# Layer norm of six attention samples by products with a constant tile instead of token rows

## The chip, the cores and the metric

One Trainium2 chip, one core of it. The time is the device time of one execution in microseconds. Five engines work in their own instruction streams and wait for each other by semaphores: PE (TensorE: matmuls and transposes), DVE (VectorE), ACT (ScalarE), POOL (GpSimd) and SyncE, whose queue issues the DMAs.

## The reference

Eight samples of 512 tokens with 512 features go through four blocks: a rotation, two modulated linear layers with a norm over the whole sample, a low-rank steering, and a transformer layer (attention with 16 heads of 32, then a feed-forward of 2048). The change touches the first norm of the last block:

```python
def layernorm(x, gamma, beta):
    mu = jnp.mean(x, axis=-1, keepdims=True)
    var = jnp.var(x, axis=-1, keepdims=True)
    return (x - mu) * jax.lax.rsqrt(var + EPS) * gamma + beta
h = layernorm(x, gamma1, beta1)
Q = (h @ Wq + bq).reshape(B, T, N_HEADS, D_HEAD).transpose(0, 2, 1, 3)
...
attn = jax.nn.softmax(scores, axis=-1)
ctx = jnp.einsum('bhqk,bhkd->bhqd', attn, V)
```

## The kernel before

A sample lies in SBUF as four tiles `x[:, j, :]` of 128 features (partitions) by 512 tokens. The norm's sums run over features, across partitions. So PE turns the sample (`tokens_in`, 16 transposes 128x128 in four groups), ACT copies the token rows out (`tokens_out`), DVE computes mean and variance (`statistics`: bn_stats, bn_aggr), POOL the reciprocal root (`prepare_rstd`), DVE normalises (`normalise`), PE turns back (`tokens_back`, four groups), ACT multiplies by gamma and adds beta (`scale_back`), and POOL cuts the result into two fp32r halves (`split`), which the three-pass products for Q, K and V read.

Attention runs over 32 groups n of four heads, four to a sample b = n // 4, two groups to a step: `first_steps(n, b)` for groups 0 and 1 of a sample, `last_steps(n, b)` for 2 and 3. In them each engine's order is written out by hand, and the norm of sample b + 1 is woven in. For a unit u of 12 in a group, PE makes scores (`score`), DVE adds the mask and takes maxima (`max_unit`), ACT takes exponentials with their sums (`exponentials`). For the transposed scores, PE makes `score_by_key`, ACT `exponentials_by_key`, POOL zeroes what is masked (`cut_later(n, half)`, four selects), PE multiplies with the values (`context`). `score_by_key(n, u)` waits for `exponentials_by_key(n, u - 2)`.

Q, K (`qk_piece`), V (`v_piece`), the steering (`st`), turned tiles (`tin`, `tb`) and the output projection share two PSUM banks. `BANK_ORDER` lists their uses in turn, even places in one bank and odd places in the other; `claim` waits until the use two places before has been taken out. DVE takes Q and K out by `qk_out` (`qk_high`, then `qk_low`). `qk_high` of the Q tile also waits for the stack DMAs of the group before (`wait_stack`), which read the tile it overwrites. SyncE's queue issues per group, in order: `max_rows(n - 1, 1)`, `stack_rows(n + 1, (0, 1))`, for group 0 `steered_out(b + 1)` (1 MB), `max_rows(n, 0)`, `stack_rows(n + 1, (2, 3))`, each `stack_rows` six DMAs.

## Time and profile before

| | us |
|---|---|
| median of 3 runs | 1609.07 |
| lowest, highest | 1608.97, 1609.23 |
| span of the profiled execution | 1610.9 |
| attention, one sample in the steady part | 82.55 |

The span runs from the first to the last instruction of one profiled execution. PE is matmuls, whose ends are modelled, so starts are the safer reading; PEld is weight loads. Steady attention lies between about 327 and 823 us, five whole samples of 82.55 us.

### The profile page before, as it was taken

How to read it: one execution, taken by the hardware profiler on the slowest of the kernel's cores; microseconds unless marked ns; L12 is line 12 of the kernel's file. 1: busy time of each engine (PE TensorE's matmuls, PEld its weight loads, DVE VectorE, ACT ScalarE, POOL GpSimd, SP SyncE). 2: the span in 40 equal slices, each digit the busy share in tenths (PEclk: the TensorE clock that was granted, in tenths of full speed). 3: DMA queues.
4: the chain of work that ended last, by engine and by line, in shares of the span. 5: the costliest groups of instructions: out<-in, count | busy, mean ns of one | idle time of the engine just before them, and what ended most of it. 6: DMA issues, size and time to landing. Idle time of an engine off the chain costs nothing.

```text
span 1610.9 us, 27177 instructions
## 1 busy us (share of the span) xinstructions
PE 1585.8 (98%) x9296; PEld 1299.5 (81%) x9298; DVE 1166.6 (72%) x2767; ACT 982.8 (61%) x2331; POOL 410.9 (26%) x605
## 2 busy tenths in 40 slices
PE   7999999999999999999999999999999999999999
PEld 4688786777777777777777688898999999999998
DVE  7999888786969686868778576785655656565643
ACT  6888766887878787878778755352433324242422
POOL 8998810313222313131312110201010110202010
PEclk8999999999999999999999999999999999999999
DMA  7042135543545444444337435866464555556361
GB/s 308 0 183 97 66 126 126 149 130 92 138 95 139 100 115 122 111 116 115 88 90 214 167 152 207 303 262 232 178 234 170 213 225 188 212 178 265 142 211 68
DMA packets 62257, 254.79 MB, mean 158 GB/s; under 512 B 10628, under 2 KB 16004, under 8 KB 46760
## 3 DMA queue, kind: packets, MB, share of 16 engines
q1 hardware_dynamic: 62120, 253.06, 48.2%
q8 instruction: 74, 1.21, 0.3%
q14 instruction: 63, 0.52, 0.1%
HBM read 153.93 MB, written 48.23 MB: 125 GB/s over the span
## 4 chain that ended last, share of the span: by engine, by line
PE 90%; POOL 3%; DMA 2%; DVE 2%; ACT 1%; issue 1%; SPq 1%; POOLq 0%; DVEq 0%; ACTq 0%
PE psum L83 24%; PE psum L84 23%; PE psum L85 23%; PE psum L1529 5%; PE psum L1549 5%; PE psum L1579 4%; PE psum L1470 1%; DMA k_weights<-w_factors 1%; PE psum L1478 1%; PE psum L2451 1%; DMA k_raw<-in_t_w 1%; POOL k_gs_square L252 1%; POOL k_gs_root L247 1%; ACT psum L1229 1%; POOL k_gs_scaled L256 1%
## 5 line engine op out<-in xcount | busy, mean ns | idle before, releaser
L1229 ACT ACTIVATE psum<-psum,b_mx 128x512 f32<-128x512 f32 (+3 forms) x512 | 258.9, 509 | 63.2 <-DVE b_mx L990 62.0
L990 DVE CUSTOM_DVE_ANT_0 psum<-psum,b_mask 128x512 f32<-128x512 f32 (+3 forms) x512 | 244.7, 506 | 53.0 <-PE psum L1529 48.1
L2398 ACT ACTIVATE k_act<-k_stack_f,k_smalls 128x512 f32<-128x512 f32 x112 | 80.9, 722 | 303.6 <-DVE k_stack_f L2237 297.1
L1241 ACT ACTIVATE k_exps<-psum 128x512 f32<-128x512 f32 (+1 forms) x384 | 194.6, 532 | 59.4 <-PE psum L1549 58.1
L864 POOL TENSOR_SCALAR_AFFINE_SELECT k_exps<-k_exps 128x256 f32<-128x256 f32 x256 | 96.4, 413 | 381.0 <-ACT k_exps L1241 379.1
L2097 POOL TENSOR_SCALAR k_result<-k_result,k_pb 128x512 f32<-128x512 f32 x32 | 59.2, 1866 | 434.9 <-DVE k_result L2156 434.9
L2216 DVE TENSOR_TENSOR k_act_lo<-k_act,k_act_hi 128x512 fp32r<-128x512 f32 x112 | 77.2, 690 | 120.6 <-ACT k_act_hi L2401 120.6
L83 PE MATMUL psum<-k_act_hi,k_w_hi 128*128 128x512 f32 x384 | 150.8, 393 | 0.0
L84 PE MATMUL psum<-k_act_lo,k_w_hi 128*128 128x512 f32 x384 | 150.5, 392 | 0.0
L85 PE MATMUL psum<-k_act_hi,k_w_lo 128*128 128x512 f32 x384 | 150.2, 391 | 0.0
L2237 DVE TENSOR_TENSOR k_raw<-psum,k_raw 128x256 f32<-128x256 f32 x168 | 70.5, 421 | 106.0 <-PE psum L85 95.4
L1529 PE MATMUL psum<-k_stack 96*128 96x512 f32 (+3 forms) x512 | 142.6, 330 | 3.1 <-DMA k_stack<-k_samples 2.0
L85 PE MATMUL psum<-k_normed,k_weights 128*128 128x512 f32 (+1 forms) x384 | 144.3, 376 | 0.0
L1549 PE MATMUL psum<-k_stack 98*128 98x512 f32 (+3 forms) x512 | 134.8, 332 | 0.6 <-ACT k_exps L1241 0.3
L83 PE MATMUL psum<-k_normed,k_weights 128*128 128x512 f32 (+1 forms) x320 | 126.0, 394 | 0.0
L84 PE MATMUL psum<-k_normed,k_weights 128*128 128x512 f32 (+1 forms) x320 | 120.0, 375 | 0.0
L1529 PEld LDWEIGHTS psum<-k_stack 96*128 96x128 f32 x512 | 93.6, 190 | 29.9 <-issue 8.8
L1549 PEld LDWEIGHTS psum<-k_stack 98*128 98x128 f32 x512 | 91.0, 189 | 27.7 <-issue 9.6
L1229 ACT ACTIVATION_READ_ACCUMULATOR psum<-psum,b_mx 128x1 f32 x512 | 108.6, 212 | 0.0
L85 PEld LDWEIGHTS psum<-k_act_hi,k_w_lo 128*128 128x128 f32 x384 | 72.1, 188 | 16.2
L85 PEld LDWEIGHTS psum<-k_normed,k_weights 128*128 128x128 f32 x384 | 73.0, 190 | 14.1
L83 PE MATMUL psum<-k_h,k_stack 128*128 128x256 f32 x294 | 82.6, 281 | 0.0
(372 smaller groups left out, 4418.2 us busy)
## 6 DMA issues: line engine op xcount, KB each, us to landing
k_stack<-w_factors SPq DMA_DIRECT2D x35, 1792.0 KB, 7.7
k_stack<-k_samples SPq DMA_DIRECT2D x384, 128.0 KB, 2.4
k_weights<-w_factors SPq DMA_DIRECT2D x17, 1792.0 KB, 7.5
x<-k_tokens SPq DMA_DIRECT2D x10, 1024.0 KB, 4.3
k_tokens<-x SPq DMA_DIRECT2D x8, 1024.0 KB, 5.1
d<-k_result SPq DMA_DIRECT2D x32, 256.0 KB, 2.9
k_raw<-x SPq DMA_DIRECT2D x8, 1024.0 KB, 4.8
k_raw<-d SPq DMA_DIRECT2D x8, 1024.0 KB, 7.1
```

The lines of the kernel that those rows point to most:

```text
L83: pe.matmul(out, w_hi, x_hi, start=start and k == 0, stop=False)
L84: pe.matmul(out, w_hi, x_lo, start=False, stop=False)
L85: last = pe.matmul(out, w_lo, x_hi, start=False, stop=stop and k == n - 1)
L864: pool.affine_select(out=own, in_=own, compare_op=ALU.is_ge, fill=0.0, base=0, pattern=[[0, 2], [1, P]], channel_multiplier=-1).then_inc(c ...
L990: last = dve.tensor_tensor_reduce(got, got, mask[:, S - width:S], -INV_SQRT_DH, -2.0 * MASKED, ALU.add, ALU.min, mx[n % 2][:, h, t:t + 1])
L1229: act.activation(sc(n, u)[:, at:at + width], sc(n, u)[:, at:at + width], ACT.Exp, bias=mx[n % 2][:, h, t:t + 1], scale=-1.0, accum_out=sum ...
L1241: act.activation(exps[n % 2][:, h, at:at + width], by_key(n, u)[:, 0:width], ACT.Exp, scale=INV_SQRT_DH).then_inc(k_act, 1)
L1529: last = pe.matmul(sc(n, u)[:, at:at + width], stack[n % 2][0:3 * DH, 2 * h, t * P:(t + 1) * P], stack[n % 2][0:3 * DH, 2 * h + 1, 0:width ...
L1549: last = pe.matmul(by_key(n, u)[:, at:at + width], stack[n % 2][0:3 * DH + 2, 2 * h + 1, j * P:(j + 1) * P], stack[n % 2][0:3 * DH + 2, 2 ...
L2216: dve.tensor_tensor(act_lo[n % 2], act_f[:], act_hi[n % 2].bitcast(F32), ALU.subtract).then_inc(act_lo_set, 1)
L2237: dve.tensor_tensor(out, got, other, ALU.add).then_inc(partial_set, 1)
L2398: act.activation(act_f[:], whole_tile, ACT.Gelu, bias=small(smalls, "b1", 2 * pair % M + second)).then_inc(pair_gelu, 1)
```

## The change

For samples 2 to 7 (`SPREAD`) the sample stays as it is. POOL adds the four feature tiles (`sample_sum`) and cuts the sum into two fp32r halves; two products with the constant tile `mean_of`, all elements 1/512, leave the mean of each token in every partition of a bank (`mean_product`). DVE subtracts it from the four tiles (`centre`), ACT squares (`squares`), POOL adds and cuts again (`square_sum`), two products give the variance (`variance_product`), ACT takes a rough reciprocal root by logarithm and exponential (`rough_rstd`), DVE makes one Newton step of it (`refine`, three instructions 128x512) and multiplies the four tiles (`multiply`), ACT applies gamma and beta (`scale_spread`), POOL splits (`split_spread`). The last norm before feed-forward and samples 0 and 1 are as before. `sample_in(b + 2)` moves from group 1 to the end of group 2 on SyncE's queue.

```diff
 BANK_ORDER = (
     (("q", 0, 1), ("k", 0, 1), ("st", 1, 0), ("v", 0, 0), ("st", 1, 1), ("st", 1, 2), ("st", 1, 3), ("v", 0, 1),
-     ("tin", 1, 0), ("q", 0, 2), ("k", 0, 2), ("tin", 1, 1), ("tin", 1, 2), ("tin", 1, 3), ("v", 0, 3),
+     ("q", 0, 2), ("mean", 1, 0), ("k", 0, 2), ("v", 0, 3), ("var", 1, 0),
      ("v", 0, 2)),
-    (("tb", 1, 0), ("q", 0, 3), ("k", 0, 3), ("tb", 1, 1), ("tb", 1, 2), ("wo", -1, 0), ("tb", 1, 3),
-     ("wo", -1, 1), ("q", 1, 0), ("k", 1, 0), ("wo", -1, 2), ("wo", -1, 3), ("pt", 2, 0), ("p", 2, 0)),
+    (("q", 0, 3), ("k", 0, 3), ("wo", -1, 0), ("wo", -1, 1), ("q", 1, 0), ("k", 1, 0), ("wo", -1, 2), ("wo", -1, 3), ("pt", 2, 0), ("p", 2, 0)),
 )
...
                 if g == 0 and b + 1 < B:
                     steered_out(b + 1)
-                if g == 1 and b + 2 < B:
-                    sample_in(b + 2)
                 if g == 3:
                     attention_out(b - 1, 2)
                 max_rows(n, 0)
                 if g == 2:
                     attention_out(b - 1, 0)
                 stack_rows(n + 1, (2, 3))
+                if g == 2 and b + 2 < B:
+                    sample_in(b + 2)
 
...
+
+        def sample_sum(b):
+
+            wait_taken(pool, ("st", b, 1))
+            pool.wait_ge(xl_set, J * b)
+            pool.tensor_tensor(tok[:, 0, :], x[:, 0, :], x[:, 1, :], ALU.add).then_inc(mean_sums, 1)
+            for j in (2, 3):
+                wait_taken(pool, ("st", b, j))
+                wait_sums(pool, b, j - 1)
+                pool.tensor_tensor(tok[:, 0, :], tok[:, 0, :], x[:, j, :], ALU.add).then_inc(mean_sums, 1)
+            wait_sums(pool, b, 3)
+            pool.tensor_copy(sums_r[:, 0, :], tok[:, 0, :]).then_inc(mean_sums, 1)
+            wait_sums(pool, b, 4)
+            pool.tensor_tensor(sums_r[:, 1, :], tok[:, 0, :], sums_r[:, 0, :].bitcast(F32), ALU.subtract).then_inc(mean_sums, 1)
+
+        def square_sum(b):
+
+            wait_squares(pool, b, 2)
+            pool.tensor_tensor(x[:, 0, :], x[:, 0, :], x[:, 1, :], ALU.add).then_inc(mean_sums, 1)
+            for j in (2, 3):
+                wait_squares(pool, b, j + 1)
+                wait_sums(pool, b, 4 + j)
+                pool.tensor_tensor(x[:, 0, :], x[:, 0, :], x[:, j, :], ALU.add).then_inc(mean_sums, 1)
+            wait_sums(pool, b, 8)
+            pool.tensor_copy(squares_r[:, 0, :], x[:, 0, :]).then_inc(mean_sums, 1)
+            wait_sums(pool, b, 9)
+            pool.tensor_tensor(squares_r[:, 1, :], x[:, 0, :], squares_r[:, 0, :].bitcast(F32), ALU.subtract).then_inc(mean_sums, 1)
+
+        def split_spread(b, j):
+            wait_squares(pool, b, J + 2 + j + 1)
+            if j == 0:
+                wait_full(pool, ("k", b - 1, G - 1))
+                wait_full(pool, ("v", b - 1, V_TILES[1][-1]))
+            pool.tensor_copy(xh[:, j, :], tok[:, j, :]).then_inc(xh_set, 1)
+            pool.wait_ge(xh_set, J * b + j + 1)
+            pool.tensor_tensor(xl[:, j, :], tok[:, j, :], xh[:, j, :].bitcast(F32), ALU.subtract).then_inc(xl_set, 1)
 
         def split(b, j):
...
                 if g == 2 and b + 1 < B:
                     for j in range(J):
-                        split(b + 1, j)
+                        split_spread(b + 1, j)
                 cut_later(n - 1, 0)
+                if g == 0 and b + 1 < B:
+                    sample_sum(b + 1)
                 if g == 1 and b + 1 < B:
-                    prepare_rstd(b + 1)
-
-        return steps(prepare_rstd, split, stacked_ones, cut_later, mask_and_low, slots)
+                    square_sum(b + 1)
+
+        return steps(prepare_rstd, mean_constants, split, stacked_ones, cut_later, mask_and_low, slots)
...
+        def centre(b, j):
+            wait_full(dve, ("mean", b, 0))
+            dve.tensor_tensor(tok[:, j, :], x[:, j, :], pj(("mean", b, 0)), ALU.subtract).then_inc(
+                mean_out if j < J - 1 else pj_dve, 1)
+
+        def refine(b):
+
+            bank, y, step = pj(("var", b, 0)), x[:, 3, :], x[:, 0, :]
+            wait_squares(dve, b, J + 2)
+            dve.scalar_tensor_tensor(step, bank, LN_EPS, y, ALU.add, ALU.mult).then_inc(pj_dve, 1)
+            wait_taken(dve, ("var", b, 0))
+            dve.scalar_tensor_tensor(step, step, -0.5, y, ALU.mult, ALU.mult).then_inc(mean_out, 1)
+            wait_spread(dve, b, J)
+            dve.scalar_tensor_tensor(step, step, 1.5, y, ALU.add, ALU.mult).then_inc(mean_out, 1)
+
+        def multiply(b, j):
+
+            wait_spread(dve, b, J + 1)
+            dve.tensor_tensor(tok[:, j, :], tok[:, j, :], x[:, 0, :], ALU.mult).then_inc(mean_out, 1)
 
...
             for k in range(3):
                 max_unit(n + 1, k)
+            shift_rows(n, 1)
+            max_unit(n + 1, 3)
+            qk_out(n + 2, 0)
+            max_unit(n + 1, 4)
             if b + 1 < B:
-                statistics(b + 1, 0)
-            shift_rows(n, 1)
-            for k in range(3, 6):
-                max_unit(n + 1, k)
+                centre(b + 1, 0)
+                centre(b + 1, 1)
+            max_unit(n + 1, 5)
             maxima_out(n, 1)
+            if b + 1 < B:
+                centre(b + 1, 2)
+                centre(b + 1, 3)
             max_unit(n + 1, 6)
             max_unit(n + 1, 7)
             shift_rows(n + 1, 0)
-            qk_out(n + 2, 0)
             qk_out(n + 2, 1)
             max_unit(n + 1, 8)
             max_unit(n + 1, 9)
-            if b + 1 < B:
-                for k in range(1, 4):
-                    statistics(b + 1, k)
             ctx_low(n - 1)
             max_unit(n + 1, 10)
             maxima_out(n + 1, 0)
-            if b + 1 < B:
-                normalise(b + 1, 0)
-                normalise(b + 1, 1)
+            values_out(b, 3)
             max_unit(n + 1, 11)
             if b + 1 < B:
-                normalise(b + 1, 2)
-                normalise(b + 1, 3)
-            values_out(b, 3)
+                refine(b + 1)
 
...
             values_out(b, 2)
             max_unit(n, 0)
             shift_rows(n - 1, 1)
-            for k in range(1, 5):
-                max_unit(n, k)
+            multiply(b + 1, 0)
+            max_unit(n, 1)
+            multiply(b + 1, 1)
+            max_unit(n, 2)
+            multiply(b + 1, 2)
+            max_unit(n, 3)
+            multiply(b + 1, 3)
+            max_unit(n, 4)
             maxima_out(n - 1, 1)
             for k in range(5, 8):
...
+        def squares(b, j):
+            if j < J - 1:
+                wait_spread(act, b, j + 1)
+            else:
+                wait_taken(act, ("mean", b, 0))
+            if j == 0:
+                act.wait_ge(x2_st, 16 * (b + 1))
+            act.activation(x[:, j, :], tok[:, j, :], ACT.Square).then_inc(mean_act, 1)
+
+        def rough_rstd(b):
+
+            y = x[:, 3, :]
+            wait_full(act, ("var", b, 0))
+            act.wait_ge(mask_made, 5)
+            wait_sums(act, b, 8)
+            act.activation(y, pj(("var", b, 0)), ACT.Ln, bias=eps[:]).then_inc(mean_act, 1)
+            wait_squares(act, b, J + 1)
+            act.activation(y, y, ACT.Exp, scale=-0.5).then_inc(mean_act, 1)
+
+        def scale_spread(b, j):
+            wait_normalised(act, b, j + 1)
+            act.activation(tok[:, j, :], tok[:, j, :], ACT.Identity, bias=small(smalls, "beta1", j),
+                           scale=small(smalls, "gamma1", j)).then_inc(mean_act, 1)
...
+            if b + 1 < B:
+                squares(b + 1, 0)
+                squares(b + 1, 1)
+                squares(b + 1, 2)
             log_sums(n + 1, 0)
             exponentials(n + 1, 6)
+            if b + 1 < B:
+                squares(b + 1, 3)
             exponentials(n + 1, 7)
-            for k in range(2, 5):
+            for k in range(2, 6):
                 exponentials_by_key(n, k)
-            if b + 1 < B:
-                tokens_out(b + 1, 1)
-            exponentials_by_key(n, 5)
-            if b + 1 < B:
...
+            exponentials_by_key(n, 9)
+            if b + 1 < B:
+                rough_rstd(b + 1)
+            exponentials_by_key(n, 10)
...
+            scale_spread(b + 1, 0)
+            exponentials(n, 3)
+            scale_spread(b + 1, 1)
+            exponentials(n, 4)
+            scale_spread(b + 1, 2)
+            exponentials(n, 5)
+            scale_spread(b + 1, 3)
...
+        def mean_product(b):
+            if b == SPREAD[0]:
+                pe.wait_ge(mask_made, 6)
+            wait_sums(pe, b, 5)
+            out = claim(("mean", b, 0))
+            pe.matmul(out, mean_of[:], sums_r[:, 0, :], start=True, stop=False)
+            pe.matmul(out, mean_of[:], sums_r[:, 1, :], start=False, stop=True).then_inc(pj_full, 1)
+
+        def variance_product(b):
+            wait_sums(pe, b, 10)
+            out = claim(("var", b, 0))
+            pe.matmul(out, mean_of[:], squares_r[:, 0, :], start=True, stop=False)
+            pe.matmul(out, mean_of[:], squares_r[:, 1, :], start=False, stop=True).then_inc(pj_full, 1)
...
-            if b + 1 < B:
-                tokens_in(b + 1, 0)
...
             score(n + 1, 3)
             qk_piece(b, 2, 3)
+            if b + 1 < B:
+                mean_product(b + 1)
...
-            if b + 1 < B:
-                tokens_in(b + 1, 1)
             score(n + 1, 9)
...
             score_by_key(n, 9)
+            if b + 1 < B:
+                variance_product(b + 1)
             v_piece(b, 2, 0)
...
             score(n, 0)
             score(n, 1)
-            tokens_back(b + 1, 0)
             score(n, 2)
...
```

Three places show how orders moved. All are in the first step of the second sample with the steady order.

DVE before, from `max_unit(n + 1, 6)` on (L990 is max_unit, L1070 shift_rows, L1002 and L1035 qk_out):

```order
L990 ISA psum,b_mx<-psum,b_mask 128x384 [waits b_s_full]
L990 ISA b_mx 128x1
L990 ISA psum,b_mx<-psum,b_mask 128x128
L990 ISA b_mx 128x1
L1070 TENSOR_TENSOR b_mx<-b_mx,b_logs 128x8 [waits b_log_set]
L1002 TENSOR_SCALAR k_samples<-psum,k_smalls 128x512 [waits b_stack_ld3,b_stack_ld2,b_pj_full,b_stack_ld1,b_stack_ld0]
L1035 SCALAR_TENSOR_TENSOR k_samples<-psum,k_smalls,k_samples 128x512 [waits b_qk_hi]
L1002 TENSOR_SCALAR k_samples<-psum,k_smalls 128x512 [waits b_pj_full]
L1035 SCALAR_TENSOR_TENSOR k_samples<-psum,k_smalls,k_samples 128x512 [waits b_qk_hi]
```

DVE of the change, from `max_unit(n + 1, 2)` on (L1059 is max_unit, L1159 shift_rows, L1071 and L1104 qk_out, L1133 centre):

```order
L1059 ISA psum,b_mx<-psum,b_mask 128x256 [waits b_s_full]
L1059 ISA b_mx 128x1
L1159 TENSOR_TENSOR b_mx<-b_mx,b_logs 128x8 [waits b_log_set]
L1059 ISA psum,b_mx<-psum,b_mask 128x512 [waits b_s_full]
L1059 ISA b_mx 128x1
L1071 TENSOR_SCALAR k_samples<-psum,k_smalls 128x512 [waits b_stack_ld3,b_stack_ld2,b_pj_full,b_stack_ld1,b_stack_ld0]
L1104 SCALAR_TENSOR_TENSOR k_samples<-psum,k_smalls,k_samples 128x512 [waits b_qk_hi]
L1059 ISA psum,b_mx<-psum,b_mask 128x384 [waits b_s_full]
L1059 ISA b_mx 128x1
L1059 ISA psum,b_mx<-psum,b_mask 128x128
L1059 ISA b_mx 128x1
L1133 TENSOR_TENSOR k_samples<-k_tokens,psum 128x512 [waits b_pj_full] x2
```

The Q tile's `qk_out` moved from behind max_unit 7 to behind max_unit 3, and the centres stand behind it.

POOL before, `cut_later(n - 1, 1)`'s last row, `cut_later(n, 0)` and `prepare_rstd`:

```order
L864 AFFINE_SELECT k_exps_91<-k_exps_91 128x2x128 [waits b_k_act]
L864 AFFINE_SELECT k_exps_91<-k_exps_91 128x2x128 x3
L864 AFFINE_SELECT k_exps_90<-k_exps_90 128x2x128 [waits b_k_act]
L864 AFFINE_SELECT k_exps_90<-k_exps_90 128x2x128 x3
L840 TENSOR_SCALAR b_var<-b_mv 128x4 [waits b_mv_set]
L842 TENSOR_TENSOR b_rstd<-b_var,k_minus_half 128x4 [waits b_var_set]
```

POOL of the change, `cut_later(n - 1, 1)`, `cut_later(n, 0)` and `square_sum`:

```order
L931 AFFINE_SELECT k_exps_93<-k_exps_93 128x2x128 [waits b_k_act]
L931 AFFINE_SELECT k_exps_93<-k_exps_93 128x2x128 x3
L931 AFFINE_SELECT k_exps_92<-k_exps_92 128x2x128 [waits b_k_act]
L931 AFFINE_SELECT k_exps_92<-k_exps_92 128x2x128 x3
L892 TENSOR_TENSOR k_tokens<-k_tokens 128x512 [waits b_mean_act]
L896 TENSOR_TENSOR k_tokens<-k_tokens 128x512 [waits b_mean_sums,b_mean_act] x2
L898 CAST k_square_sums<-k_tokens 128x512 [waits b_mean_sums]
L900 TENSOR_TENSOR k_square_sums<-k_tokens,k_square_sums 128x512 [waits b_mean_sums]
```

Two instructions on 128x4 became five on 128x512 behind the same cut.

PE before, from `maxima(n + 1, 0)` (L1565) and `score_by_key(n, 9)` (L1549) to V's last tile:

```order
L1565 MATMUL psum<-k_ident,b_mx 8x128 [waits b_cl_set,b_max_set,b_shift_set]
L1549 MATMUL psum<-k_stack 128x512 [waits b_k_act]
L83 MATMUL psum<-k_weights,k_normed 128x512 [waits b_pj_act]
L84 MATMUL psum<-k_weights,k_normed 128x512
L85 MATMUL psum<-k_weights,k_normed 128x512
```

PE of the change at the same place (L1702, L1686):

```order
L1702 MATMUL psum<-k_ident,b_mx 8x128 [waits b_cl_set,b_max_set,b_shift_set]
L1686 MATMUL psum<-k_stack 128x512 [waits b_k_act]
L1615 MATMUL psum<-k_square_sums,b_mean_of 128x512 [waits b_pj_dve,b_mean_sums]
L1616 MATMUL psum<-k_square_sums,b_mean_of 128x512
L83 MATMUL psum<-k_weights,k_normed 128x512 [waits b_pj_dve]
L84 MATMUL psum<-k_weights,k_normed 128x512
L85 MATMUL psum<-k_weights,k_normed 128x512
```

The two variance products stand between them, with a wait for POOL's sums (`b_mean_sums`).

## Rows read from the trace of the kernel before

**Rows 1.** The page, part 1: busy us (share of the span) xinstructions of each engine.

```profile
PE 1585.8 (98%) x9296; PEld 1299.5 (81%) x9298; DVE 1166.6 (72%) x2767; ACT 982.8 (61%) x2331; POOL 410.9 (26%) x605
```

**Rows 2.** Stretches of one sample: engines' busy us (xcount), then PEclk, DMA share, GB/s.

```profile
410.15:492.70 82.55, 82.40 (x503) 63.59 (x503) 65.21 (x199) 65.02 (x198) 20.71 (x42) 1.00 0.47 116
...
657.80:740.35 82.55, 82.35 (x503) 63.57 (x503) 65.20 (x199) 64.99 (x198) 20.72 (x42) 1.00 0.46 116
```

**Rows 3.** Timeline of PE, 422 to 437 us: start, us, engine, line, operation, tiles, form, count.

```profile
422.95 0.40 PE L84 MATMUL psum<-k_normed,k_weights 128*128 128x512 f32 x1
423.18 0.39 PE L85 MATMUL psum<-k_normed,k_weights 128*128 128x512 f32 x1
...
423.88 0.44 PE L83 MATMUL psum<-k_normed,k_weights 128*128 128x512 f32 x1
...
430.44 0.51 PE L1549 MATMUL psum<-k_stack 98*128 98x384 f32 x2
...
430.95 0.60 PE L1470 MATMUL psum<-k_ident,k_tokens 128*128 128x128 f32 x4
431.31 0.48 PE L1529 MATMUL psum<-k_stack 96*128 96x512 f32 x1
431.62 0.28 PE L1549 MATMUL psum<-k_stack 98*128 98x256 f32 x1
...
436.62 0.39 PE L83 MATMUL psum<-k_weights,k_normed 128*128 128x512 f32 x1
```

**Rows 4.** Timeline of DVE, 414 to 429 us.

```profile
414.56 2.08 DVE L1047 SCALAR_TENSOR_TENSOR k_tokens<-psum,k_pb,k_tokens 128x512 f32<-128x512 f32 x3
...
423.25 0.69 DVE L990 CUSTOM_DVE_ANT_0 psum<-psum,b_mask 128x512 f32<-128x512 f32 x1
...
427.97 0.74 DVE L1002 TENSOR_SCALAR k_samples<-psum,k_smalls 128x512 fp32r<-128x512 f32 x1
428.75 0.75 DVE L1035 SCALAR_TENSOR_TENSOR k_samples<-psum,k_smalls,k_samples 128x512 fp32r<-128x512 f32 x1
```

**Rows 5.** Timeline of SyncE's queue, 417 to 425 us.

```profile
417.18 3.23 SPq L787 DMA_DIRECT2D k_stack<-k_maxima  x4
420.50 4.06 SPq L779 DMA_DIRECT2D k_stack<-k_samples  x6
```

**Rows 6.** DMA issues of 420 to 425 us: tiles, count, KB each, median us to landing.

```profile
k_stack<-k_samples SPq DMA_DIRECT2D x6, 128.0 KB, 2.5
```

**Rows 7.** Groups of DVE, one sample, then (L2237) later: busy us, mean ns | idle before.

```profile
L1052 DVE BATCH_NORM_STATS2 b_st<-k_samples 128x6 f32<-128x512 f32 x4 | 2.7, 675 | 0.0
...
L1059 DVE TENSOR_SCALAR k_samples<-k_samples,b_mv,b_rstd 128x512 f32<-128x512 f32 x4 | 2.0, 541 | 0.0
...
L1054 DVE BATCH_NORM_AGGREGATE b_mv<-b_st 128x2 f32<-128x6 f32 x4 | 0.7, 183 | 0.1
...
L2237 DVE TENSOR_TENSOR k_stack_f<-psum,k_raw 128x512 f32<-128x512 f32 x111 | 75.6, 682 | 5.5 <-PE psum L85 4.3 <-ACT k_act L2398 1.2
```

**Rows 8.** Timeline of ACT, 431 to 433 us.

```profile
431.59 0.60 ACT L1253 ACTIVATE k_samples<-psum 128x512 f32<-128x512 f32 x1
432.09 0.38 ACT L1241 ACTIVATE k_exps<-psum 128x256 f32<-128x256 f32 x1
```

**Rows 9.** Timeline of POOL at 432 us.

```profile
432.53 1.49 POOL L864 TENSOR_SCALAR_AFFINE_SELECT k_exps<-k_exps 128x256 f32<-128x256 f32 x4 [7.11 <-ACT k_exps L1241]
```

**Rows 10.** Groups of POOL in one sample, columns as in rows 7.

```profile
L851 POOL TENSOR_TENSOR k_normed<-k_samples,k_normed 128x512 fp32r<-128x512 f32 x4 | 5.1, 1287 | 0.3
L849 POOL CAST k_normed<-k_samples 128x512 fp32r<-128x512 f32 x4 | 2.5, 612 | 10.7 <-issue 7.0 <-ACT k_samples L1258 3.7
```

**Rows 11.** Short stretches with the granted clock (PEclk), columns as in rows 2.

```profile
256.00:257.80 1.80, 0.40 (x3) 0.13 (x1) 1.68 (x3) 0.83 (x4) 0.00 (x0) 1.00 0.00 0
259.20:262.50 3.30, 3.30 (x9) 2.73 (x10) 3.24 (x12) 1.76 (x5) 0.00 (x0) 0.50 0.88 192
263.00:266.00 3.00, 2.58 (x12) 1.75 (x11) 2.33 (x11) 2.03 (x9) 0.00 (x0) 1.00 0.21 46
```

More of the change, by code:

```diff
@@ L596 @@
 AFTER = B
+SPREAD = range(2, B)
+TURNED_AT = {b: k for k, b in enumerate(b for b in range(B + 1) if b not in SPREAD)}
 U_TILES = ((T - 1,), (T - 2, 0), (1,))
@@ L1354, in last_steps @@
             log_sums(n - 1, 1)
-            scale_back(b + 1, 0)
-            for k in range(6):
-                exponentials(n, k)
+            exponentials(n, 0)
+            exponentials(n, 1)
+            exponentials(n, 2)
+            scale_spread(b + 1, 0)
[5 more added lines that the diff above has]
+            scale_spread(b + 1, 3)
             exponentials_by_key(n - 1, 0)
@@ L2778, in gpsimd_head @@
     att.stacked_ones()
+    att.mean_constants()
     att.prepare_rstd(1)
```

81 lines of the change are left out of this document (45 added, 36 removed).

## The prediction

> **What bounds the kernel now.** I read the table of busy shares first, then the stretches of one sample, then the timelines of the engines around the edited places. TensorE (PE) is busy 98% of the span [rows 1]; in the steady stretches of attention one sample takes 82.55 us, in five stretches alike, and PE is busy for 82.40 of them, VectorE (DVE) and ScalarE (ACT) for 65, GpSimd (POOL) for 21 [rows 2]. That the matmuls really follow each other, and do not only overlap on paper, is read from the starts: 422.95 and 423.18 us, one 512-column product each 0.23 us [rows 3]. So in this part each microsecond of work taken from PE is worth a microsecond, and each wait added on PE costs one. The Trainium skill ("Trainium Kernel Development and Optimization", Performance Expectations) warns that matmul busy time says little of how near a kernel is to its limit, and prefers the weight loads' share; that is 77% here (63.59 of 82.55). If that meant slack in PE, less than the term below would come back from the removed work; the starts decide against it.
>
> **What is removed from PE.** Per sample 8 groups of four transposes. One group starts at 430.95 and the next product at 431.31, and that product then takes 0.31 instead of 0.23 us, because its weights come late [rows 3]: 0.36 + 0.08 = 0.44 us a group, 3.5 us a sample. Added are four 512-column products, 0.23 each: 0.9. Net -2.6 us a sample, and 6 samples have it: -15.6 us. That is all that the change can give; three waits stand against it.
>
> **First wait: the bank of K.** Q, K and the other projections take turns in two banks, and each claims the bank of the one before last. Before, K's third tile (first product at 423.88 [rows 3]) claims the bank of the first turned token tile, which ACT has long emptied. Now it claims the bank of Q's own third tile, since only the mean stands between them. So `qk_piece(b, 2, 4)` waits for DVE to run `qk_out(n + 2, 0)`, a pair of 0.74 and 0.75 us (427.97 to 429.50 [rows 4]). The change moves that pair forward, behind `max_unit(n + 1, 3)`, which runs from 423.25 to 423.94 [rows 4]. But its first half also waits for all four `stack_ld` of group n + 1, since it overwrites what those DMAs read. SyncE issues the last six of them from 420.50 to 424.56, right behind the four row DMAs of 417.18 that end at 420.41, one every 0.65 us [rows 5]; from issue to landing is 2.5 us [rows 6]. The last is issued at about 423.96 and lands at 426.4. The queue ahead of it is the same after the change. So the pair ends at 426.4 + 1.5 = 427.9. PE comes to K at 423.88 - 0.44 (a group gone) + 0.46 (the two mean products) = 423.90. Stall: 4.0 us. In the kernel before the same pair began at 427.97 and nobody waited for it. Behind the blocked pair on DVE stand `max_unit(n + 1, 4)`, all four `centre`, and with them ACT's squares. If the rows landed early only the pair itself would count: Q is complete at 423.6 - 0.44, the pair would end at 424.9 and the stall be 1.0. Bounds 1.0 to 4.5; I take 4.0, since the landing is read, not guessed.
>
> **Second wait: exponentials by key.** After that pair DVE has, in order, max_unit 4, two `centre`, max_unit 5, the maxima, two `centre`, max_unit 6 and 7. A `centre` reads a bank and an SBUF tile; the nearest row is 0.68 us [rows 7], a 512-column max_unit is 0.69 [rows 4], and the list adds up to about 5.8 us. ACT runs `squares` (nearest row 0.60 [rows 8]) ahead of the max_unit results and then `exponentials_by_key(n, 2)`, so that ends about 7.1 us after the pair. PE comes to `score_by_key(n, 4)`, which waits for it, after 6.6 us (423.88 to 430.44 [rows 3]); another short wait follows at unit 6. I take 1.1 us; bounds 0 and 2.
>
> **Third wait: the variance.** POOL's `square_sum` stands behind `cut_later(n, 0)`, and that waits for `exponentials_by_key(n, 5)`. In the trace: `score_by_key(n, 5)` starts on PE at 431.62 [rows 3], ACT takes it 432.09 to 432.47 [rows 8], POOL cuts 432.53 to 434.02 [rows 9]. Then `square_sum`: three adds, a cast, a subtraction. The same shape costs POOL 1.29 us with two inputs and 0.61 for a cast [rows 10], and about 0.08 from one to the next: 4 x 1.37 + 0.69 = 6.2 us. From the start of `score_by_key(n, 5)` that is at least 0.3 + 0.4 + 1.6 + 6.2 = 8.5 us. PE comes to `variance_product`, in the place before 436.62 [rows 3], after 436.62 - 431.62 - 2 x 0.44 = 4.1 us, some 0.3 more with the short wait of the paragraph above. Stall: 4.1 us. This difference doesn't depend on the stalls before it, since both sides hang on the same unit. If adds cost no more than the cast, it would be 4.1 - 4 x 0.68 = 1.4; bounds 1.4 and 5. I take 4.1, because the 1.29 is the same engine, shape and number of inputs. The Trainium skill ("GPSIMD Engine Reference", 3.1 and 4.1) speaks against the change here: two-input elementwise work belongs on VectorE and is about twice as slow on GpSimd, with 4497 ns for 2048 fp32 columns. By that page an estimate for 512 is 1.12 us and the stall 3.4; the trace agrees in kind and decides the number.
> The first sum on POOL is not late: it can start when the second `steered` tile is written, about 415.3 (the first of the three that start from 414.56, 0.69 us apart [rows 4]), lasts 6.2 to 421.5, and PE asks at about 423.0, after the product of 423.18 less 0.44.
>
> **The clock and the backlog.** PE has not stood still for 4 us anywhere in attention before. Where it was busy for 0.40 of the 1.80 us from 256.00, the granted clock was 0.50 (1.2 GHz) soon afterwards, in the stretch 259.20 to 262.50, and 1.00 (2.4 GHz) again from 263 on [rows 11]; PE did nine products there in 3.3 us, where it does 14 at full clock. One such fall costs about 1.6 us. After the variance ACT has a logarithm and an exponential (0.6 each) and the held-back `exponentials(n + 1, 10)` to run, DVE the three `refine` (0.75 each, as the pair of [rows 4]) and then four `multiply` between its max_units (0.68 each [rows 7]); I count 0.7 to 1.5 us of waits at scores 4 and 7 of the next group, which overlap the slow clock. Two stalls, two falls, partly hidden: 2.5 us a sample together; bounds 0 and 5.
> DVE itself: added 8 x 0.68 + 3 x 0.75 = 7.7, removed 4 x 0.86 + 4 x 0.54 = 5.6 [rows 7], so 67 of 82 us, not the bound. ACT: +1.5 likewise. POOL: +11, to 31. The splits of the normalised sample have the same prices as before and no longer wait for turned tiles between them: nothing there. `sample_in` moves one slot later on SyncE's queue, behind the stack rows of the third group; its megabyte is first used near the end of the fourth, a group (20 us) later: nothing.
>
> **Sum.** -2.6 + 4.0 + 1.1 + 4.1 + 2.5 = +9.1 us a sample, +54.6 for six. The profiled execution has a span of 1610.9 us against a median of 1609.07; the sum is a difference within the first and I add it to the median: 1609.1 + 54.6 = 1663.7. A sample would take about 91.6 us instead of 82.55.
>
> **Rivals.**
> A, the two long waits alone: ACT and DVE catch up in the stalls and the clock stays: -2.6 + 4.0 + 4.1 = +5.5, 1642. For it: 65 of 82 us busy on both. Against: the falls after far shorter idle times.
> B, POOL adds at the cast's price, or the rows land early, so that one of the long waits nearly goes: -2.6 + 4.0 + 1.4, or -2.6 + 1.0 + 4.1, i.e. +2.6 to +2.8 a sample, 1625.
> C, faster: the change does what its work says. Neither K's bank nor the variance is late on PE, because the six DMAs or the cuts are in fact issued earlier once their PE producers run earlier. Then -15.6: 1593.5. It decides at 2.6 us of waits a sample; above that the kernel is slower. Against: the variance alone needs 8.5 us where PE leaves 4.1.
> D, worse: the backlog makes DVE the bound from K's bank to the next group's scores (each max_unit late by a further `centre` or `multiply`), and both falls cost in full: -2.6 + 4.5 + 2 + 5 + 5 = +13.9, 1692.
> That the change is without effect is not open: PE's order and banks change in all six samples.
>
> **How the numbers follow.** Forecast 0.60, A 0.20, B 0.08, C 0.05, D 0.05, something near zero 0.02. A difference of 0.2% (3.2 us) is about what can be told from none. Faster 0.05, same 0.02, slower 0.93. The range 1626 to 1686 leaves out C, D and part of B: under 2 in 10.
>
> **What would show it.** For the first wait: PE idle of about 4 us before the product on the bank of K's third tile, DVE's pair waiting for the DMA into the stack. For the third: PE idle of about 4 us before the products with k_square_sums, released by POOL; POOL's adds at 1.3 us. For the clock: granted clock below 1.00 in the stretches of attention. The sample's period gives the sum: 91.6 forecast, 88 for A, 80 for C. I am wrong if the adds are cheap, if the pair is not held by the DMAs, or if PE's idle time is not lost because other work there had slack.

## The result and the profile after

| | before | after |
|---|---|---|
| median, us | 1609.15 (4 runs) | 1689.29 (4 runs) |
| lowest, highest | 1608.97, 1610.13 | 1689.02, 1692.07 |
| span of the profiled execution | 1610.9 | 1687.4 |
| attention, one sample | 82.55 | 96.1, then 94.1 to 95.3 |

The ratio is 1.0496, 95% interval 1.0479 to 1.0513: slower by 80.1 us. The sign was forecast; the size was not (1663.7), and 1689.3 lies above the range (1626 to 1686). The two spans differ by 76.5; the execution of before whose trace is shown ran some 3 us over its median. Of the 76.5, the six changed samples take 74.0 (the product that starts at 327.65 and 822.92 before starts at 325.68 and 895.01 after), the last sample 4.4, and the part ahead of them gives 2.0 back.

Part 1 of the page of after (columns as in [rows 1]):

```profile
PE 1601.9 (95%) x9128; PEld 1299.4 (77%) x9130; DVE 1174.1 (70%) x2761; ACT 992.6 (59%) x2343; POOL 471.0 (28%) x655
```

Stretches of after (columns as in [rows 2]): one sample (the third changed one, which all lines below are from unless said otherwise), then the time behind each of its two long waits.

```profile
487.60:582.30 94.70, 85.30 (x476) 63.83 (x475) 66.39 (x197) 66.66 (x200) 31.03 (x50) 0.95 0.41 101
533.70:538.50 4.80, 4.80 (x13) 3.95 (x14) 4.55 (x13) 3.54 (x11) 0.00 (x0) 0.50 0.01 4
552.20:555.70 3.50, 3.50 (x11) 2.90 (x11) 1.21 (x4) 2.88 (x8) 0.00 (x0) 0.51 0.00 0
```

Against [rows 2] the sample is 12.15 us longer. PE idles for 9.4 of it, and its busy time *rose* by 2.9 although 27 instructions are gone: in the two short stretches the granted clock is half (1.2 GHz), and each product takes 0.43 us from start to start instead of 0.23.

**The first wait.** The timeline of PE (start and length in us; in brackets the idle time ahead and what ended it):

```profile
533.66 0.79 PE L83 MATMUL psum<-k_normed,k_weights 128*128 128x512 f32 x1 [3.93 <-DVE k_samples L1104]
534.25 0.63 PE L84 MATMUL psum<-k_normed,k_weights 128*128 128x512 f32 x1
```

The timeline of SyncE's queue:

```profile
522.85 3.22 SPq L809 DMA_DIRECT2D k_stack<-k_maxima  x4
526.18 3.88 SPq L801 DMA_DIRECT2D k_stack<-k_samples  x6
```

And that of DVE:

```profile
532.07 0.75 DVE L1071 TENSOR_SCALAR k_samples<-psum,k_smalls 128x512 fp32r<-128x512 f32 x1 [2.77 <-DMA k_stack<-k_samples]
532.85 0.75 DVE L1104 SCALAR_TENSOR_TENSOR k_samples<-psum,k_smalls,k_samples 128x512 fp32r<-128x512 f32 x1
```

This is the chain as it was forecast from [rows 3 to 6]: rows issued until 530.06, the last lands at 531.9 (2.4 us after its issue), DVE has stood idle for 2.77 us, the pair takes 1.5, K starts at 533.66.

**The third wait.** The timeline of POOL:

```profile
544.04 1.48 POOL L931 TENSOR_SCALAR_AFFINE_SELECT k_exps<-k_exps 128x256 f32<-128x256 f32 x4 [13.32 <-ACT k_exps L1334]
545.49 1.29 POOL L892 TENSOR_TENSOR k_tokens<-k_tokens 128x512 f32<-128x512 f32 x1
546.92 2.69 POOL L896 TENSOR_TENSOR k_tokens<-k_tokens 128x512 f32<-128x512 f32 x2
549.67 0.61 POOL L898 CAST k_square_sums<-k_tokens 128x512 fp32r<-128x512 f32 x1
550.36 1.26 POOL L900 TENSOR_TENSOR k_square_sums<-k_tokens,k_square_sums 128x512 fp32r<-128x512 f32 x1
```

And that of PE:

```profile
547.61 0.48 PE L1686 MATMUL psum<-k_stack 98*128 98x512 f32 x1
551.68 0.50 PE L1615 MATMUL psum<-k_square_sums,b_mean_of 128*128 128x512 f32 x1 [3.59 <-POOL k_square_sums L900]
```

From 545.49 to 551.62 POOL needs 6.1 us, at the 1.29 and 0.61 us that [rows 10] gave for other tiles.

**The rest.** The timeline of ACT in the third group:

```profile
565.70 0.81 ACT L1375 ACTIVATE k_samples<-k_samples,k_smalls 128x512 f32<-128x512 f32 x1
566.40 1.08 ACT L1334 ACTIVATE k_exps<-psum 128x512 f32<-128x512 f32 x2
```

The product on PE that waits for it:

```profile
567.05 0.39 PE L1686 MATMUL psum<-k_stack 98*128 98x256 f32 x1 [1.09 <-ACT k_exps L1334]
```

And in the last sample, which has no such norm, the timeline of DVE:

```profile
911.42 0.75 DVE L1071 TENSOR_SCALAR k_samples<-psum,k_smalls 128x512 fp32r<-128x512 f32 x1 [1.98 <-DMA k_stack<-k_samples]
```

And of PE:

```profile
914.85 0.50 PE L1666 MATMUL psum<-k_stack 96*128 96x384 f32 x2 [2.58 <-ACT psum L1322]
```

K's bank is free there, but `qk_out(n + 2, 0)` has been moved forward all the same. It blocks DVE until the rows have landed, `max_unit(n + 1, 4)` stands behind it, and a score waits 2.6 us for that unit's exponentials.

**The ledger of one sample.** Taking the start of each product in both traces, and how far the difference grows from one to the next (sample from 492.7 before, 515.8 after):

| | us |
|---|---|
| work removed and added, with short waits of 0.3 us or less | -1.7 |
| wait before K's third tile | +4.1 |
| half clock behind it | +2.2 |
| wait before the variance products | +3.8 |
| half clock behind it | +1.5 |
| waits of the third group for exponentials (0.4, 0.3, 1.3) and small change | +2.3 |
| sum | +12.2 |

The half clock is a price of this sample, not a fixed one. Two stretches of other samples of after, behind the first wait of the fifth and behind the variance wait of the first, which was 3.59 us long like this one's:

```profile
723.60:729.70 6.10, 6.10 (x17) 5.09 (x18) 5.01 (x15) 4.76 (x14) 0.00 (x0) 0.50 0.01 2
361.90:368.00 6.10, 6.10 (x17) 4.94 (x17) 2.42 (x5) 3.65 (x11) 1.19 (x3) 0.50 0.26 56
```

Over the six samples the half clock behind the first wait lasts 3.1 to 6.1 us, behind the variance wait 3.2 to 3.5 and once 6.1.

### The profile page after: what moved, and what is told of

Read it like the earlier page. It is cut to its first block, busy times and chain, and to the rows that moved or that the text cites. A ratio compares the mean times of both kernels' runs of the same rounds, so it can differ in the third digit from the quotient of the medians.

```text
span 1687.4 us, 26933 instructions
## 1 busy us (share of the span) xinstructions
PE 1601.9 (95%) x9128; PEld 1299.4 (77%) x9130; DVE 1174.1 (70%) x2761; ACT 992.6 (59%) x2343; POOL 471.0 (28%) x655
## 4 chain that ended last, share of the span: by engine, by line
PE 75%; DVE 6%; POOL 5%; SPq 4%; ACT 4%; DMA 3%; issue 2%; DVEq 0%; POOLq 0%; ACTq 0%
PE psum L83 21%; PE psum L84 20%; PE psum L85 20%; PE psum L1716 4%; PE psum L1686 4%; PE psum L1666 3%; SPq L801 2%; SPq L809 2%; DMA k_stack<-k_samples 2%; ACT psum L1322 2%; ACT k_samples L1375 1%; ACT k_exps L1334 1%; POOL k_tokens L896 1%; DVE psum L1059 1%; DMA k_raw<-in_t_w 1%
## 5 line engine op out<-in xcount | busy, mean ns | idle before, releaser
L1059 DVE CUSTOM_DVE_ANT_0 psum<-psum,b_mask 128x512 f32<-128x512 f32 (+3 forms) x512 | 243.8, 506 | 73.2 <-PE psum L1666 67.5
L83 PE MATMUL psum<-k_normed,k_weights 128*128 128x512 f32 (+1 forms) x320 | 130.2, 407 | 25.1 <-DVE k_samples L1104 25.1
L1686 PE MATMUL psum<-k_stack 98*128 98x512 f32 (+3 forms) x512 | 140.2, 341 | 9.5 <-ACT k_exps L1334 8.4
L85 PE MATMUL psum<-k_normed,k_weights 128*128 128x512 f32 (+1 forms) x384 | 146.9, 382 | 0.0
L1686 PEld LDWEIGHTS psum<-k_stack 98*128 98x128 f32 x512 | 94.6, 196 | 42.6 <-ACT k_exps L1334 15.4
L84 PE MATMUL psum<-k_normed,k_weights 128*128 128x512 f32 (+1 forms) x320 | 122.4, 383 | 0.0
L83 PEld LDWEIGHTS psum<-k_normed,k_weights 128*128 128x128 f32 x320 | 62.8, 196 | 34.3 <-DVE k_samples L1104 26.3
L85 PEld LDWEIGHTS psum<-k_normed,k_weights 128*128 128x128 f32 x384 | 74.6, 194 | 14.9
```

Of the source, the lines that this page charges most:

```text
L83: pe.matmul(out, w_hi, x_hi, start=start and k == 0, stop=False)
L84: pe.matmul(out, w_hi, x_lo, start=False, stop=False)
L85: last = pe.matmul(out, w_lo, x_hi, start=False, stop=stop and k == n - 1)
L1059: last = dve.tensor_tensor_reduce(got, got, mask[:, S - width:S], -INV_SQRT_DH, -2.0 * MASKED, ALU.add, ALU.min, mx[n % 2][:, h, t:t + 1])
L1686: last = pe.matmul(by_key(n, u)[:, at:at + width], stack[n % 2][0:3 * DH + 2, 2 * h + 1, j * P:(j + 1) * P], stack[n % 2][0:3 * DH + 2, 2 ...
```

## The experiments

Theory 1 is the ledger: two waits, each with a slow clock behind it. Its rivals: the waits are a symptom of engines that are late anyway; the slow clock has another cause.

**One wait at a time, and both.** The first wait is taken away by a second buffer for the Q and K tiles, the third by shorter adds. In this and the following edits three dots stand for lines left out.

```diff
+    qk_other = late("qk_other", [P, J, S], F32, WO + TILE)
+    qk_at = lambda n: qk_other[:] if n % 2 and n > G else qk
...
-                wait_stack(dve, n - 1, range(HG))
+                wait_stack(dve, n - 1 if n < G + 2 else n - 2, range(HG))
```

> The changed kernel with a second buffer for the Q and K tiles in the place of the low half of the output projection's weights, which is left out (its product reads the high half twice); the first half of the Q pair then waits for the stack rows of two groups before, not one. Theory 1 (a wait on the tensor engine costs itself and the slow clock behind it): the wait before K's third tile falls from 3.9 to about 1.0 us (the pair of 1.5 us behind a finished Q), the slow stretch behind it (2.2 us) goes: -5.1 to -5.3 us a sample, 1657 to 1659 us. Theory 2 (the vector and scalar engines are behind anyway and the wait only moves to the scores): under 3 us a sample, over 1671.

Measured: 1661.9 us, some 3 above theory 1 and 9 below theory 2 (before, run beside this kernel and the next three: 1611.4; beside the others 1609.7 to 1611.4; differences to after, whose before was 1609.2, carry some 2 us of that). The wait before K is 1.0 us. The last sample, which has no norm, lies only 1.1 us over before instead of 4.4: its wait was for the stack rows too.

```diff
...
-                pool.tensor_tensor(x[:, 0, :], x[:, 0, :], x[:, j, :], ALU.add).then_inc(mean_sums, 1)
+                pool.tensor_tensor(x[:, 0, 0:64], x[:, 0, 0:64], x[:, j, 0:64], ALU.add).then_inc(mean_sums, 1)
```

> The changed kernel with the three adds of the squares on 64 of 512 columns (7/8 of that sum is left out), all else and every wait as it was. Theory 1: three adds are each about 1.1 us shorter, the wait before the variance products falls from 3.8 to about 0.6 us, and the slow clock behind it (1.5 us) goes with it: -4.8 us a sample, 1660 us. Theory 2 (the slow clock is not the wait's): -3.2 us a sample, 1670.

Measured: 1662.6 us; theory 1 said 1660, theory 2 1670. And with both edits:

> Both edits (second Q and K buffer without the low half of the output projection's weights; adds of the squares on 64 columns). Theory 1: the two gains add, -10 us a sample, 1629 us, and what is left over the kernel before is about 2 us a sample of waits on exponentials. Theory 2 (one backlog behind both): clearly less than the sum, over 1640.

Measured: 1635.8 us, between theory 1 (1629) and theory 2 (over 1640). Single edits -27.4 and -26.7, together -53.5: within the spread of the runs (2 to 5 us) the two prices add. The waits of PE in both_waits (us in total, times, longest):

```profile
PE psum L1687 <- ACT k_exps L1335: 11.9, 19, 1.1
PE psum L83 <- DVE k_samples L1106: 6.0, 6, 1.0
PE psum L1616 <- POOL k_square_sums L902: 4.4, 6, 0.7
```

And one sample of it as a stretch:

```profile
470.90:557.10 86.20, 81.57 (x476) 60.79 (x475) 66.07 (x197) 66.53 (x200) 27.91 (x50) 1.00 0.44 112
```

The waits are down to 1.0 and 0.7 us, the clock is full, and a sample takes 86.2 us. That is still 3.65 over before, where 2 had been expected: by the starts of the products, waits for exponentials of 0.7, 0.8, 0.3 and 1.3 us are left. They depend neither on a long wait nor on the clock; the norm's instructions stand ahead of the exponentials on ACT and of the maxima on DVE, in the third group above all.

**The clock.** Work without effect in the place of the first wait:

```diff
             out = claim(("mean", b, 0))
+            for _ in range(8):
+                pe.matmul(out, mean_of[:], sums_r[:, 0, :], start=True, stop=False)
+                pe.matmul(out, mean_of[:], sums_r[:, 1, :], start=False, stop=True)
```

> The changed kernel with the two products of the mean made nine times over instead of once: 16 more products of 0.23 us, 3.7 us of work where the tensor engine stands still for 3.9 us. If the clock falls because the engine stood still: the products cost nothing, the slow stretch of 2.2 us goes, 1676 us. If the slow stretch comes from something else (the queue of work behind, or a limit on power): no gain, 1689 or more.

Measured: 1687.5 us (runs from 1684.5 to 1691.8), 1.8 less than after, where 13 had been expected: not told from no gain. The stretches behind the two waits in this kernel (columns as in [rows 2]):

```profile
531.60:536.00 4.40, 4.35 (x25) 3.53 (x25) 4.33 (x13) 3.63 (x12) 0.00 (x0) 1.00 0.00 0
...
548.40:554.20 5.80, 5.80 (x16) 4.70 (x16) 2.42 (x5) 3.65 (x11) 0.85 (x2) 0.51 0.23 50
```

Both answers are half right. The clock behind the first wait is full once PE works through it, so standing still was what lowered it. But the gain was given back: in four of six samples the last stack rows took 3.2 to 3.8 us to land instead of 2.4, so K still waited 1.1 us or more; the exponentials by key were 0.6 us later; and behind the variance wait, unchanged at 3.6 us, the slow stretch is 5.8 us instead of 3.5. That last part can't be put down to the products, since after itself has 6.1 us behind the same wait in its first sample. And in the last sample the wait of 2.6 us (ended at 914.85 in after, at 912.92 here) left the clock full in after and halved it here. First after, then fill_wait:

```profile
914.90:922.00 7.10, 6.84 (x55) 4.51 (x56) 5.07 (x17) 6.18 (x20) 1.48 (x4) 1.00 0.14 29
```

```profile
912.90:919.00 6.10, 6.08 (x31) 3.14 (x35) 2.82 (x9) 3.52 (x12) 0.00 (x0) 0.50 0.02 4
```

A slow spell has no fixed price that one could take off the sum.

**The bank and the early pair, in the kernel before.** Layer norm by transposes; only the first turned tile goes between Q and K, and Q's bank is emptied earlier (`qk_out(n + 2, 0)` behind `max_unit(n + 1, 3)`), as in the change.

```diff
-     ("tin", 1, 0), ("q", 0, 2), ("k", 0, 2), ("tin", 1, 1), ("tin", 1, 2), ("tin", 1, 3), ("v", 0, 3),
+     ("q", 0, 2), ("tin", 1, 0), ("k", 0, 2), ("tin", 1, 1), ("tin", 1, 2), ("tin", 1, 3), ("v", 0, 3),
...
```

> The kernel before, layer norm by transposes as it was, with one thing of the change: K's third tile claims the bank of Q's third tile (the first turned tile goes between them), and Q's bank is emptied behind max_unit 3. If the bank order alone makes the first wait: K waits 4 us for the pair behind the stack rows, with 2.2 us of slow clock, +6 us in six samples, 1645 us. If the wait needs the norm's new work (products late, sums on POOL): within 5 us of before.

Measured: 1653.9 us, ratio 1.0274 (1.0258 to 1.0289), 44 us over before. The timeline of PE:

```profile
522.13 0.50 PE L83 MATMUL psum<-k_normed,k_weights 128*128 128x512 f32 x1 [3.96 <-DVE k_samples L1035]
```

And the stretch behind that wait:

```profile
522.10:526.50 4.40, 4.37 (x14) 3.65 (x15) 3.07 (x11) 2.17 (x8) 0.00 (x0) 0.61 0.00 0
```

The same wait of 4 us and a clock of 0.61 over the 4.4 us behind it, about 6.0 us a sample, without one instruction of the new norm. The last sample pays here too, 5.9 us, and there the list is as before: that part is the early pair's. So more than half of the change's loss comes with K's place in the list and the early pair together. The place alone, with the pair where it was, was not run.

**The variance alone later.** The product goes behind V's last tile, root, refinement and multiplies with it.

```diff
-            if b + 1 < B:
-                variance_product(b + 1)
             v_piece(b, 2, 0)
...
                 v_piece(b, 2, k)
+            if b + 1 < B:
+                variance_product(b + 1)
```

> The changed kernel with the variance product behind V's last tile and the root and the multiplies a few units later; K's bank as in the change. Theory 1: the wait of 3.8 us and its slow clock of 1.5 us go, the others stay: -5.4 us a sample, 1657 us. Theory 2 (the time is only lent, and the scores of the third group wait for the vector engine instead): less than half of that, over 1673.

Measured: 1676.4 us. Theory 2 holds here: the wait is down to 0.4 us, but 13 of the 32 us are all that comes back. A sample is 2.7 us shorter; PE now waits for exponentials in the third group five times, by 0.6, 0.7, 0.5, 0.9 and 1.0 us. Small sums had shortened POOL's work without moving any; moving it puts it where DVE and ACT are needed.

**Everything later.** Mean product behind K, variance product, root and scaling in the third group behind K's fourth tile.

```diff
-     ("q", 0, 2), ("mean", 1, 0), ("k", 0, 2), ("v", 0, 3), ("var", 1, 0),
-     ("v", 0, 2)),
-    (("q", 0, 3), ("k", 0, 3), ("wo", -1, 0), ("wo", -1, 1), ("q", 1, 0), ("k", 1, 0), ("wo", -1, 2), ("wo", -1, 3), ("pt", 2, 0), ("p", 2, 0)),
+     ("q", 0, 2), ("k", 0, 2), ("mean", 1, 0), ("v", 0, 3), ("v", 0, 2)),
+    (("q", 0, 3), ("k", 0, 3), ("var", 1, 0), ("wo", -1, 0), ("wo", -1, 1), ("q", 1, 0), ("k", 1, 0), ("wo", -1, 2), ("wo", -1, 3), ("pt", 2, 0), ("p", 2, 0)),
...
```

> The whole computation of the changed kernel with three things in other places: the mean product stands behind K's third tile (so K claims a bank that is long empty), the variance product, its root and the scaling stand 13 us later, in the next step (POOL's six us are over by then), and POOL splits behind its cut. If only the two long waits and the clock behind them cost time: no wait before K or the variance, clock full, about 1 us a sample of waits on exponentials against 2.6 us of work removed, 1599 us, faster than before. If the norm's work on the vector and scalar engines costs the scores what it no longer costs there: waits of 2 to 4 us at the third group's scores, 1607 to 1617 us.

Measured: 1663.7 us, neither of the two (1599, or 1607 to 1617). The bank rule bites again, one claim further on: now the mean waits for Q's pair, and the variance for that of Q's fourth tile. The timeline of PE:

```profile
525.87 0.47 PE L1604 MATMUL psum<-k_token_sums,b_mean_of 128*128 128x512 f32 x1 [1.78 <-DVE k_samples L1103]
```

The stretch behind it, after the one behind the same wait a sample earlier:

```profile
435.40:439.00 3.60, 3.60 (x40) 1.91 (x39) 1.55 (x3) 0.96 (x3) 0.00 (x0) 1.00 0.02 5
...
526.20:530.10 3.90, 3.90 (x24) 1.26 (x26) 1.52 (x3) 0.98 (x2) 0.00 (x0) 0.56 0.01 4
```

A wait of 1.8 us was followed by a half clock in four of six samples, with 0.56 over the 3.9 us here; of the contexts that follow, four products of 512 columns side by side took 0.85 us from start to start instead of 0.43. In the other two samples the same 1.78 us left the clock full. The Trainium skill ("TensorE: Matmul & The Clock Gate", Part 1) has the clock at 1.2 GHz after idleness and at 2.4 after work; the trace agrees in kind (0.56 behind this wait), and shows that the length of the wait alone does not decide it.

**Those waits moved away.** The mean product goes behind the contexts, the third group's Q pair two maxima earlier, the context's low half ahead of the multiplies.

```diff
             maxima_out(n - 1, 1)
-            for k in range(5, 8):
-                max_unit(n, k)
+            max_unit(n, 5)
             qk_out(n + 1, 0)
+            max_unit(n, 6)
+            max_unit(n, 7)
...
```

> The kernel of the run before it (mean product behind K, variance 13 us later) with its four remaining waits moved out of the way: the mean product behind the contexts, the third group's Q pair two maxima earlier, the context's low half ahead of the multiplies, gamma and beta one exponential earlier. If those waits of 1.6 to 2.2 us and the half clock behind two of them were all that cost time: no wait over 1 us in a steady sample, clock full, 81 to 82 us a sample, 1598 to 1606 us. If the norm's extra work on three engines always leaves some score waiting: 84 us a sample or more, over 1617.

Measured: 1624.4 us, the second of the two (over 1617), ratio 1.0080 (1.0066 to 1.0095); a steady sample takes 83.8 us at full clock. Two thirds through the sample PE is 1.2 us *ahead* of before, then it loses 2.5. The cause stands on DVE and POOL. The timeline of DVE:

```profile
543.21 0.78 DVE L1148 TENSOR_TENSOR k_samples<-k_samples,k_tokens 128x512 f32<-128x512 f32 x1
544.58 0.68 DVE L1148 TENSOR_TENSOR k_samples<-k_samples,k_tokens 128x512 f32<-128x512 f32 x1
545.90 1.74 DVE L1148 TENSOR_TENSOR k_samples<-k_samples,k_tokens 128x512 f32<-128x512 f32 x1
548.23 1.80 DVE L1148 TENSOR_TENSOR k_samples<-k_samples,k_tokens 128x512 f32<-128x512 f32 x1
```

And that of POOL:

```profile
545.81 1.29 POOL L908 TENSOR_TENSOR k_normed<-k_samples,k_normed 128x512 fp32r<-128x512 f32 x1
547.04 1.07 POOL L906 CAST k_normed<-k_samples 128x512 fp32r<-128x512 f32 x1
548.19 1.28 POOL L908 TENSOR_TENSOR k_normed<-k_samples,k_normed 128x512 fp32r<-128x512 f32 x1
```

The same multiply takes 0.68 us, or 1.74 and 1.80 where POOL's subtraction has begun just before it.

**Is it POOL?** POOL's splits on 64 of 512 columns, the cast shown here and the subtraction likewise:

```diff
-            pool.tensor_copy(xh[:, j, :], tok[:, j, :]).then_inc(xh_set, 1)
+            pool.tensor_copy(xh[:, j, 0:64], tok[:, j, 0:64]).then_inc(xh_set, 1)
...
```

> later2 with POOL's cast and subtraction of the normalised tiles on 64 of 512 columns (7/8 of both halves is left out). If the multiplies of 1.7 to 1.8 us were long because POOL read at the same time: all four at 0.7 us, the two waits behind them (1.1 and 0.5 us) gone, some 2 us a sample, 1612 us. If they were long for another reason (their operands, scale_spread on ACT): still 1.7 us, within 4 us of 1624.

Measured: 1609.2 us, 15 less than later2; ratio to before 0.9989 (0.9979 to 0.9999). The timeline of DVE:

```profile
541.41 0.69 DVE L1148 TENSOR_TENSOR k_samples<-k_samples,k_tokens 128x512 f32<-128x512 f32 x1
542.67 0.68 DVE L1148 TENSOR_TENSOR k_samples<-k_samples,k_tokens 128x512 f32<-128x512 f32 x1
```

And one sample as a stretch:

```profile
466.80:548.50 81.70, 80.81 (x477) 60.66 (x476) 66.31 (x197) 66.08 (x201) 26.62 (x50) 1.00 0.47 118
```

All four multiplies at 0.7 to 0.8 us, 81.7 us a sample. It was POOL's work at the same time, and its subtraction above all: beside the full casts alone, in a run below, no multiply took over 1.1 us. In a steady sample this is worth 2.2 us, some 13 of the 15 in six. The first changed sample is 4.4 us shorter: there later2 has a half clock behind a wait of 1.7 us, and short_split has none behind one of 2.0. The Trainium skill ("GPSIMD Engine Reference", 1. Specifications) has GpSimd share its way into SBUF with VectorE and names VectorE instructions with two SBUF inputs as those in contention. The trace agrees: the multiply has two, while `centre`, whose second input is a bank, took 0.68 us beside POOL's adds in later2.

**Three orders against the contention.** Variance before Q's fourth tile and multiplies spread out:

```diff
...
             score(n, 2)
+            variance_product(b + 1)
             for k in range(4):
                 qk_piece(b, 3, k)
...
```

> Again the whole computation. Against later2, the variance product stands before Q's fourth tile (behind the third score of the third group), the vector engine takes the last subtraction of the squares from POOL, and the root's three steps and the four multiplies are spread over ten maxima, so that they end before POOL splits most tiles. If later2's last 2 us a sample come from the multiplies of 1.8 us that run beside POOL's splits: multiplies of 0.7 us, 81 to 82 us a sample, 1599 to 1606 us. If the vector engine is the bound in the third group, whatever the order: scores there wait 1 to 3 us, 1611 to 1622 us.

Measured: 1619.1 us; 83.8 us a sample. Multiplies of 1.4 and 1.0 us are left, and by the starts of the products PE is later by 0.4 to 1.0 us, six times. Then, from later2 again, POOL's subtraction given to DVE:

```diff
-            pool.tensor_tensor(xl[:, j, :], tok[:, j, :], xh[:, j, :].bitcast(F32), ALU.subtract).then_inc(xl_set, 1)
+            dve.tensor_tensor(xl[:, j, :], tok[:, j, :], xh[:, j, :].bitcast(F32), ALU.subtract).then_inc(xl_set, 1)
...
```

> The whole computation. Against later2, the vector engine takes the subtraction of the normalised tiles too (POOL keeps only the casts), so that no long two-input instruction of POOL runs beside the four multiplies, and the next sample's megabyte is loaded one store later. As the run with short splits: multiplies of 0.7 us, 81.6 us a sample, 1605 us, faster than before by 4 us. If four more subtractions (2.8 us) make the vector engine late, or the cast alone blocks it: 83 us or more a sample, over 1611.

Measured: 1621.0 us where 1605 was hoped for; no multiply over 1.1 us, but the products wait for DVE's subtractions. And with these ahead of the projection's results:

```diff
             multiply(b + 1, 3)
-            attention_result(b - 1, 0)
             spread_low(b + 1, 0)
+            attention_result(b - 1, 0)
...
```

> The whole computation; later4 with the four subtractions of the vector engine ahead of the two results of the output projection instead of between and behind them. In later4 the four products on the normalised tiles waited 0.8, 0.3, 0.45 and 0.8 us for them. If only the order is late: these waits halve at least, about 82 us a sample, 1606 to 1611 us, even with before or a little faster. If the vector engine has no room left here: other waits in their place, 84 us, over 1616.

Measured: 1616.9 us, ratio 1.0044 (1.0028 to 1.0060). One sample as a stretch:

```profile
465.70:548.90 83.20, 80.96 (x477) 60.63 (x475) 68.58 (x201) 66.03 (x201) 27.40 (x46) 1.00 0.46 116
```

DVE is busy for 68.6 us of 83.2 and yet late where it counts. This has the lowest median of the whole versions, though its runs (1616.0 to 1621.9) overlap with those of later3 (1617.2 to 1624.7), and it does not beat the kernel before. Whether 81.7 us a sample can be had with all the work done stays open; only short_split, which leaves most of the splits out, reached it.

## Why the prediction was wrong

The reading of the kernel held, the sum did not. By its own steps:

- **Removed work**, -2.6, and **second wait**, 1.1. Together forecast -1.5, measured -1.7, partly by luck. The second wait was one of 0.26 us; that leaves about -2.0 for the work, since most removed groups gave back 0.36 to 0.45 us and the four products took 0.46 to 0.56 a pair. Two misses of 0.6 to 0.8 us cancel.
- **First wait**, 4.0: measured 4.1, by the chain named, from rows to pair to K. The landing time could be taken from before, since what stands ahead of it on the queue had not changed. two_qk also found the lower bound, 1.0.
- **Third wait**, 4.1: measured 3.8. The doubt whether adds might be as cheap as the cast was settled at 1.29 us.
- **Clock and backlog**, 2.5 together, bounds 0 and 5: this step failed. The clock alone took 3.7 (2.2 and 1.5) and the backlog 2.3: 6.0. The text had two falls at 1.6, which makes 3.2, and 0.7 to 1.5 of waits, 3.9 to 4.7 in all, and then took off 1.4 to 2.2 for an overlap that nothing in the profile showed. The waits and the slow stretches lie one behind the other on PE, the engine that bounds: in the ledger they add up.
- **The backlog** itself, 0.7 to 1.5, was too small as well. It had been read as what the variance's wait leaves behind. But both_waits has 3.1 us of waits for exponentials with full clock and short waits, 2.4 of them in the third group, where after has 2.3: it stems from where the instructions stand in DVE's and ACT's orders. That both are busy for only 65 of 82 us said nothing about it.
- **What was left out**: the last sample (4.4 us). The text read the early `qk_out` as part of the norm, but the diff moves it in every sample. Six samples were counted where one step runs in seven. With second buffers (two_qk) the last sample cost 1.1.
- The first changed sample took 96.1 us, not 94 to 95. Its first wait was 5.1 us, since three of the six stack rows took 3.8 to 4.1 us to land, and behind the variance wait the half clock lasted 6.1 us. Neither was in the sum.
- Rival B's lower figure is 2.5 by its own terms, not 2.6; nothing hangs on it.

Rival D (+13.9 a sample) had the size, with every bound at its upper end; the measured +12.2 lies between forecast and D. It had been given 0.05, and the range stopped short of it. As a faster kernel (rival C) the idea is not wrong in itself: short_split, which leaves most of the splits out, shows that some 0.9 us a steady sample would be there. The point given for it, 2.6 us of waits a sample, held: after has 7.9 us of long waits alone.

## What to carry to other kernels

Where one engine is saturated, price a new wait as its length *plus* what the slow clock takes behind it (as a range: the same wait was followed by 3.2 us of half clock or by 6.1), and give no discount for overlap unless a row shows what it would overlap with. When uses of two alternating buffers are taken out of a list, write down for every use left what it now waits for: in this kernel one new place in that list, with the pair moved for it, cost 44 us. And look through the diff for moves that also act where the rest of the change does not.
